# Moving the head products to the end of TensorE's turn in a fused attention and mixture-of-experts layer

## The reference

```python
# attention: 16 query heads of 128, 8 key/value heads, so a key/value head serves a pair of query heads
q = layernorm(x) @ Wq ; k = ctx @ Wk ; v = ctx @ Wv
attn = softmax(where(mask, q @ k.T / sqrt(128), -inf))
x = x + (attn @ v) @ Wo
# feed-forward: 32 experts in 4 groups; the best 2 groups, then the best 4 experts of a row
scores = sigmoid(layernorm(x) @ gate_w.T)
out = sum over the 4 chosen experts of weight * (silu(r @ w1) * (r @ w3)) @ w2, 128 slots for each expert
out = out + (silu(r @ shared_gate) * (r @ shared_up)) @ shared_down
x = x + out
```

## Time and profile before

| | |
|---|---|
| median of 3 runs | 1640.18 us (1640.02 to 1640.26) |
| the profiled execution: its own time | 1641.88 us |
| its span (first to last instruction) | 1639.70 us |
| PE busy | 1604.7 us, 98% |
| DVE, ACT, POOL busy | 1219.1 us, 846.7 us, 797.3 us |
| attention loop, by the first and last `scores` | 17.7 to 1202.5 us |

### The profile page before, as it was taken

The page is one execution under the profiler, slowest core; times in us unless marked ns, Lnnn a source line. Parts: engine busy times, 40 slices in busy tenths (PEclk is TensorE's granted clock), DMA queues, the critical chain, the costliest instruction groups (busy, mean ns, idle before and its releaser), DMA issues. The chain is left out here.

```text
span 1639.7 us, 35025 instructions
## 1 busy us (share of the span) xinstructions
PE 1604.7 (98%) x12199; PEld 1149.5 (70%) x12199; DVE 1219.1 (74%) x3520; ACT 846.7 (52%) x2090; POOL 797.3 (49%) x1096
## 2 busy tenths in 40 slices
PE   8999999999999999999999999999999999999996
PEld 5767777777777777777777677777777666666663
DVE  7988787887778787777887787878766256766773
ACT  6764545454454454454545445445433156666672
POOL 3443646455564646464554646464346433333323
PEclk9999999999999999999999999999999999999999
DMA  8765454454555545445445454444466478988935
GB/s 262 182 155 108 105 97 111 77 112 79 119 96 117 109 86 105 97 111 91 124 81 120 92 117 111 88 111 83 103 215 193 103 208 218 272 244 221 268 67 65
DMA packets 399662, 218.28 MB, mean 133 GB/s; under 512 B 348400, under 2 KB 356592, under 8 KB 399488
## 3 DMA queue, kind: packets, MB, share of 16 engines
q1 hardware_dynamic: 383024, 189.71, 46.6%
q0 software_dynamic: 15904, 25.29, 9.3%
q10 hardware_dynamic: 560, 1.05, 0.2%
HBM read 91.87 MB, written 40.80 MB: 81 GB/s over the span
## 5 line engine op out<-in xcount | busy, mean ns | idle before, releaser
L967 ACT ACTIVATE arena<-arena,neg_max 128x256 f32<-128x256 f32 x512 | 253.7, 496 | 378.4 <-DVE neg_max L1276 378.4
L711 POOL TENSOR_SCALAR arena<-arena,prob_scale 128x256 f16<-128x256 f32 x384 | 185.3, 498 | 478.5 <-DVE prob_scale L1285 436.1
L1648 PE MATMUL ps_query<-xn_both,arena 128*128 128x256 f16 x1024 | 279.2, 273 | 0.7 <-DMA xn_both<-xn_half 0.7
L1650 PE MATMUL ps_query<-xn_both,arena 128*128 128x256 f16 x1024 | 279.2, 273 | 0.0
L1649 PE MATMUL ps_query<-xn_both,arena 128*128 128x256 f16 x1024 | 279.2, 273 | 0.0
L1276 DVE CUSTOM_DVE_ANT_0 arena<-ps_score,mask_add 128x256 f32<-128x256 f32 x512 | 186.3, 420 | 80.8 <-PE ps_score L1650 80.8
L1291 DVE SCALAR_TENSOR_TENSOR arena<-arena,prob_scale 128x256 f16<-128x256 f32 x384 | 239.6, 673 | 7.6 <-POOL arena L711 7.6
L1648 PE MATMUL ps_out<-arena,o_t 128*128 128x512 f16 x512 | 194.2, 379 | 0.6 <-DVE o_t L1296 0.5
L1650 PE MATMUL ps_out<-arena,o_t 128*128 128x512 f16 x512 | 194.2, 379 | 0.0
L1649 PE MATMUL ps_out<-arena,o_t 128*128 128x512 f16 x512 | 194.2, 379 | 0.0
L1296 DVE SCALAR_TENSOR_TENSOR o_t<-ps_head,o_t 128x512 f16<-128x512 f32 x128 | 88.4, 690 | 89.0 <-ACT o_t L980 89.0
(11 more groups left out here) (337 smaller groups left out, 4068.2 us busy)
## 6 DMA issues: line engine op xcount, KB each, us to landing
arena<-w SPq DMA_DIRECT2D x96, 512.0 KB, 6.1
out_rows_dram<-weight_in POOLq DMA_DIRECT2D x32, 256.0 KB, 5.3
x_in<-x SPq DMA_DIRECT2D x15, 512.0 KB, 3.8
out_rows_dram<-x SPq DMA_DIRECT2D x30, 256.0 KB, 2.4
xn_rows<-xn_half SPq DMA_DIRECT2D x15, 512.0 KB, 3.1
x2t_kept<-xn_both SPq DMA_DIRECT2D x12, 512.0 KB, 2.9
ctx_in<-ctx_t SPq DMA_DIRECT2D x16, 256.0 KB, 3.0
weight_in<-wq SPq DMA_DIRECT2D x8, 512.0 KB, 5.0
```

The costliest lines, as they stand in the source:

```text
L711: pool.tensor_scalar(p_rows[:, c, 0, :], probs[:, c, :], prob_scale[:, c:c + 1], 1.0, ALU.mult, ALU.mult).then_inc(norm_hi, 1)
L967: act.activation(probs[:, c, :], probs[:, c, :], ACT.Exp, bias=neg_max[:, c:c + 1], scale=-1.0, accum_out=prob_sum[:, c:c + 1]).then_inc(e ...
L1648: pe.matmul(dst, a.hi, b.hi, start=start and n == 0, stop=False)
L1650: m = pe.matmul(dst, a.lo, b.hi, start=False, stop=stop and n == len(pairs) - 1)
```

## The change

TensorE's turn becomes: `scores(i)`, `query(i + 1, 0)`, filler, `query(i + 1, 1)`, filler, `key(i + 1)`, `project(i - 2)`, `attend(i - 1)`. The loops of PE, ACT and DVE run one turn more to finish the last projection. On DVE the head's low half (`head_low(i - 2)`) comes right behind the maxima, and the low halves of query and key come ahead of `probs_low`, which is no longer cut in two. On ACT `head_high(i - 2)` begins the turn and `query_high` comes ahead of `scale_last`. Side work moves to a later turn, mostly by one: the value tiles to turns 1 to 3, the gate to turn 4, the ranks to turn 7, `turn_xn2` to turn 3. `xn2_rest` moves from ahead of turn 2's `prob_scales` to behind turn 3's `probs_low`. `record(z, 0)` and `record(z, 1)` move from turn 7 and the next item's turn 0 to turns 0 and 1 of the item after it, so that all eight indirect DMAs of item 14 come after the loop.

```diff
@@ def first, def second (fillers; b > 0)
-            if j == 1:
+            if j == 2:
                 return ("value", a, 0, 1) if a < B else None
-            return {3: ("gate", z), 6: ("rank", z)}.get(j)
+            return ("rank", z) if j == 7 and b == B - 1 else None
...
-            if j < 3:
-                return ("value", a, *((0, 0), (1, 0), (1, 1))[j]) if a < B else None
+            if 1 <= j < 4:
+                return ("value", a, *((0, 0), (1, 0), (1, 1))[j - 1]) if a < B else None
+            if j == 4 or j == 7 and b < B - 1:
+                return ("gate" if j == 4 else "rank", z)
             return None
@@ pe_program
-            for i in range(TURNS + 1):
+            for i in range(TURNS + 2):
...
-                else:
-                    piece(1)
-                if i:
-                    attend(i - 1)
                 if i + 1 < TURNS:
                     query(i + 1, 1)
...
                 if i >= TURNS - 1:
-                    piece((i - TURNS + 1) * 2)
-                if i:
-                    project(i - 1)
+                    piece(i - TURNS + 1)
+                if i >= 2:
+                    project(i - 2)
+                if 1 <= i <= TURNS:
+                    attend(i - 1)
@@ act_program
+                if i >= 2:
+                    head_high(i - 2)
                 if i < TURNS:
                     exps(i)
...
-                if i:
-                    head_high(i - 1)
+                if i + 1 < TURNS:
+                    query_high(i + 1)
                 if i < TURNS:
                     scale_last(i)
...
-                if j == 4 and b + 1 < B and i < TURNS:
+                if j == (5 if b else 4) and b + 1 < B and i < TURNS:
                     for t in range(TB):
                         xn_high(b + 1, t)
-                if i + 1 < TURNS:
-                    query_high(i + 1)
...
-                if j == 1 and b and i < TURNS:
+                if j == 3 and b and i < TURNS:
                     for t in range(TB):
                         xn2_high(b - 1, t)
@@ dve_program (the side work's new turns are in the text above)
                 if live:
                     maxima(i)
+                if i >= 2:
+                    head_low(i - 2)
...
+                if i + 1 < TURNS:
+                    query_low(i + 1)
                 if live:
-                    probs_low(i, range(0, CELLS // 2))
...
+                    filler(second(b, j), ps_fill[0])
+                if i + 1 < TURNS:
                     key_low(i + 1)
                 if live:
-                    probs_low(i, range(CELLS // 2, CELLS - 1))
...
+                    probs_low(i, range(CELLS - 1))
...
+                if j == 3 and routed:
+                    for t in range(TB):
+                        xn2_rest(z, t)
...
+                if j == 5 and live and a < B:
+                    xn_rest(a, 0)
+                if j == 5 and routed:
                     choose_5()
                     choose_6()
@@ sync_program
-                if j == 2 and b:
+                if j == 3 and b:
                     for t in range(TB):
                         turn_xn2(b - 1, t)
@@ pool_program
-                if j == 7 and b:
-                    record(z, 0)
                 if j == 0 and b > 1:
+                    record(b - 2, 0)
+                if j == 1 and b > 1:
                     record(b - 2, 1)
...
-            record(z - 1, 1)
+            for t in range(TB):
+                record(z - 1, t)
```

More of the change, by code:

```diff
@@ L792, in pool_program @@
                     halve_ident()
-                if j == 1 and b:
+                if j == 2 and b:
                     inv_std(1, z, x1_stats, x1_rstd, x1_normed)
@@ L1475, in dve_program @@
                 live, routed = i < TURNS, i < TURNS and b > 0
-                if j == 1 and routed:
+                if j == 2 and routed:
                     residual(z, 1)
@@ L1479, in dve_program @@
                     maxima(i)
+                if i >= 2:
+                    head_low(i - 2)
                 for n in split_amid.get(i, ()):
                     weight_low(n)
-                if j == 1 and routed:
+                if j == 0 and b > 1:
+                    dve.wait_ge(*own.now())
+                    pick(position)
+                    find_slots(b - 2)
+                if j == 2 and routed:
                     for t in range(TB):
                         x1_stats_row(z, t)
[L1485 to L1488, removed]
+                if j == (4 if b else 3) and live and a < B:
                     for t in range(TB):
                         x_stats_row(a, t)
-                if j == 4 and routed:
+                if j == 5 and routed:
                     choose_2()
@@ L1494, in dve_program @@
                     choose_4()
-                if j == 5 and routed:
-                    choose_7()
-                    choose_8(z)
                 if j == 6 and live and a < B:
-                    for t in range(TB):
-                        xn_rest(a, t)
+                    xn_rest(a, 1)
                 if j == 7 and routed:
-                    dve.wait_ge(*own.now())
-                    pick(position)
-                    find_slots(z)
+                    choose_10()
+                    choose_11(z)
                 if live:
@@ L1507, in dve_program @@
                     filler(first(b, j), ps_fill[1])
-                else:
-                    piece(1)
                 if i == 0:
                     value_low(ps_fill[1], 0, 0, 0)
-                late_head = live and first(b, j) is not None and first(b, j)[0] == "value"
-                if i and not late_head:
-                    head_low(i - 1)
+                if i + 1 < TURNS:
+                    query_low(i + 1)
                 if live:
-                    probs_low(i, range(0, CELLS // 2))
-                if i and late_head:
-                    head_low(i - 1)
-                if i == 0:
-                    query_low(i + 1)
+                    filler(second(b, j), ps_fill[0])
+                if i + 1 < TURNS:
                     key_low(i + 1)
                 if live:
-                    probs_low(i, range(CELLS // 2, CELLS - 1))
-                if 0 < i < TURNS - 1:
-                    query_low(i + 1)
-                early_key = live and second(b, j) is not None and second(b, j)[0] == "value"
-                if i + 1 < TURNS and early_key:
-                    key_low(i + 1)
-                if live:
-                    filler(second(b, j), ps_fill[0])
-                if 0 < i < TURNS - 1 and not early_key:
-                    key_low(i + 1)
-                if j == 1 and b == B - 1 and live:
+                    probs_low(i, range(CELLS - 1))
+                if j == 2 and b == B - 1 and live:
                     x1_norm(z)
@@ L1559, in dve_program @@
                     ctx_low(b + 2)
-                if j == 0 and b:
-                    residual(z, 0)
             z = B - 1
-            residual(z, 1)
+            for t in range(TB):
+                residual(z, t)
             for t in range(TB):
```

31 lines of the change are left out of this document (16 added, 15 removed).

## The result

The changed kernel takes 1652.32 us (median of 4 runs, 1651.62 to 1653.68), the kernel before 1640.10 on the same chip: a ratio of 1.0076, 95% interval 1.0058 to 1.0093. It is slower, and by more than the 0.2% that can be told from nothing. I had forecast 1634.2.

A forecast was written before the change was run, and what follows sets the result against it. PE, busy for 98% of the span, bounds the kernel, so only its waits count. -11.5 - 3.0 + 3.5 + 3.0 + 2.0 = -6.0 us on 1641.88 gives 1635.9; that execution was 1.7 above the median, so 1634.2; range 1625 to 1644.

The forecast's parts named there:

- The bound now, and what the change takes away: PE's waits in the loop: 11.5 us for late transposes and 3.0 us for late keys at turn 0 would go.
- New waits +3.5: In the loop, late landings at the gate and the chains behind it add 3.5 us, between 0 and +9.
- The gate: Turn 4: operands land at 13.3, wanted at 13.72, slack 0.4; two late landings at 15 gates cost 2.4 us.
- The chain behind SP's queue: Turn 3's probabilities' transposes land at 6.4 in turn 4, wanted at 7.8; attend and DVE's turn 6 chain cost about 1 us.
- the slack of 0.4: Turn 6: DVE's low half of the head ends at 4.2, and the projection wants it at 4.59.
- The signs of being wrong: PE waiting at ps_fill for a DMA in most items, or at ps_out for DVE, or landings late more often.
- DVE's low halves nearer to 470: DVE's low halves of probabilities, mostly behind POOL's work, take near 470 ns each, 1.3 us for three.
- The start, +3.0: Program start: one projection deeper, 2.6 us, plus 0.4 for DVE's catching up in turn 3; between 0 and +4.
- Behind the loop, +2.0: Item 14's eight indirect DMAs on POOL delay the chain to add_shared by 2.0 us, between 0 and 5.2.
- The gate becomes a wait at every item: Rival: xn2_rest's transposes land later, gate stops PE in each of 15 items, 12 us, 1643.8; chance 0.16.
- A blocked DVE: Rival: DVE's choosing steps in turn 5 blocked by POOL's x_norm, 16 us over 15 items, 1650; chance 0.04.
- From 1630 to 1637: Whole kernel: the likeliest case's time span in us, with the bounds of the three costs.

The follow-up runs named there:

- gate_early: Changed kernel with xn2's high halves right behind turn 3's exponentials on ACT and its low halves right behind turn 3's probability scales on DVE; 1634.68 us, ratio 0.9969.
- queue: gate_early with the gate's second transpose on SP held until turn 2's attend ends, its rows' store next, both ahead of turn 3's probabilities' transposes; 1664.08 us.
- head_first: Changed kernel with head_low(i - 2) ahead of maxima(i) on DVE; 1650.35 us, ratio 1.0066.
- warm: Changed kernel with eight matmuls of zeros (512 columns each) at the end of each of PE's first two turns; 1651.80 us, ratio 1.0073.
- tail: Changed kernel with the four indirect DMAs of the first half of item 14's record behind POOL's split of piece 2, not piece 5; 1655.50 us.
- start: gate_early with the low half of weight chunk 7 ahead of turn 1's probs_low on DVE; 1638.89 us, ratio 0.9987.
- tail2: gate_early with the four indirect DMAs of the first half of item 14's record behind POOL's split of piece 1; 1635.74 us, ratio 0.9965.
- shift: Changed kernel with 64 matmuls of 8 columns of zeros ahead of the first key product on PE; 1660.23 us, ratio 1.0111.

## Why the prediction was wrong

**The bound now, and what the change takes away.** Right in kind and size: 11.5 us of waits for transposes and 3.0 of late keys were predicted, and the loop of the kernel before is 14.5 us longer than the dense one of gate_early. That it fits to a tenth is luck: place by place the two come to 10.9 and 2.9, and item 1 has other waits. Scores follow the matmul ahead of them directly at turn 0, and one wait at `ps_head` is left.

**"New waits +3.5", between 0 and +9.** This is the step that failed: they are 17.6 us in the loop, 17.6 - 3.5 = 14.1 of the 15.7 by which the sum missed (+9.7 in place of -6.0). It failed in two parts.

*The gate.* The times on DVE and SP were right to 0.2 us, with a slack of about 0.6 for landings of 2.7. I took two late ones. There are four in 15, and waits that I had not looked for (DVE 0.5 to 0.7 late in items 5, 8 and 12; item 15, whose turn 3 has no filler): 9.0 us in place of 2.4. Each item offers two transposes, and a late one costs 1.3 to 1.7.

*The chain behind SP's queue.* I wrote that the probabilities' transposes of turn 3 land at 6.4 in turn 4 and that `attend` wants them at 7.8. The engine that matters is POOL, which may not overwrite their source before. For `x_norm` I allowed for a delay of this kind (not before 9.3 + 1.3 in turn 4, where an ordinary turn has POOL through at 7.3), and for nothing else. DVE's low halves of turn 4 wait for POOL too, and behind them the gate's evaluation and the maxima of turn 5: this path I had not followed. Nor had I followed a late landing along it. With none, and DVE in time, POOL starts 6.6 to 6.9 into turn 4, much as my 6.4 says; in the six items with a landing of over 4 us it starts at 7.7 to 8.6, and the median of all is 7.6. In turn 6 the slack of 0.4 was not there: the projection waits 0.2 to 0.5 in 11 items, and the scores in 5. The chain cost 8.8 us in place of "about 1". queue shows that the delay on SP is enough to make these waits, head_first that swapping the two steps at their end only moves them.

**The signs of being wrong.** One that I had named came: landings are late more often than before, 41 against 27 over 4 us (last section).

**"DVE's low halves nearer to 470."** Too low: the median is 610 ns, from 684. POOL's halves and DVE's still overlap in most turns. It did not hurt the gate (`xn2_rest` starts 8.3 into turn 3, forecast 8.4), but it stands in the chain of turns 4 and 5 above, where three took 1.84 us at 892.82. POOL's first high half came a little later than forecast too: in turn 4 of gate_early 4.9 to 5.7 and not 4.6 to 4.7.

```profile
L1293 DVE SCALAR_TENSOR_TENSOR arena<-arena,prob_scale x384: 471/610/910, 25.6 to 1212.6; 128x256 f16<-128x256 f32 x192
```

**The start, +3.0.** 4.3 (2.6 for the projection, 1.7), a little over the upper bound. Scores of turn 3 start at 45.56 and not near 44: DVE's weight chunk 7 stands behind low halves that now come in one piece. The drop of the clock beside it costs next to nothing (warm, tail), and moving the chunk only moves the gap (start).

**Behind the loop, +2.0.** 2.3, by the mechanism named: the eight DMAs, PE's wait of 2.4 at piece 12, and the wait near 1294 at 4.0 as forecast.

**The rivals.** "The gate becomes a wait at every item" (1643.8) was the right side but the wrong shape: it is a wait at half of the items, and as much again comes from the queue behind it. "A blocked DVE" (1650) is near in time and wrong in cause. Beside POOL's `x_norm`, DVE's `beats` took 0.19 us as it does elsewhere, but the step ahead of it, `group_score`, was held for a short time:

```profile
896.39 4.13 POOL L682 TENSOR_SCALAR weight_in<-x_in,mean_var,rstd 128x512 f32<-128x512 f32 x2
...
898.65 0.58 DVE L1324 TENSOR_TENSOR group_score<-group_top 128x8 f32<-128x8 f32 x1
899.27 0.19 DVE L1330 TENSOR_TENSOR beats<-group_score 128x32 f32<-128x32 f32 x1
```

In the 14 items where it starts 0.19 to 0.26 us after the second instruction of `x_norm` it takes 0.52 to 0.59, and each time it ends 0.78 after the start of that one; in the kernel before, where it starts 0.9 us or more after it, it takes 0.17. So 0.4 us of DVE went there in turn 5, behind the maxima and the head's half of that turn and ahead of its scales, and not up to 1.6; in gate_early the same happens in three items and no wait follows. The rule of the Trainium skill (SBUF — State Buffer, "Who interferes with whom"), by which the later one is blocked until the first is finished, is borne out by neither row: POOL's instruction runs for 2.07.

**A bound that was worked out wrongly.** "From 1630 to 1637" does not follow from the bounds of the three costs. They give 1640.2 - 14.5 = 1625.7 and, with 18.2 added, 1643.9, which is the range that I stated at the end.

**The order itself.** gate_early is the change with two steps of side work placed elsewhere, and it takes 1634.68 us. So the moved products do win what I had counted; the side work's new place gave it away. gate_early and tail2 beat the kernel before, by 0.3% each, and the changed one by about 1%.

## What to carry to other kernels

When a transfer is queued behind another one, list everyone who waits for its landing, not only the product that reads it: the engine that may not overwrite its source comes first here. Follow a late start through every turn until the chain has slack again, since the loss comes out one or two turns later, on another engine. And place a transfer whose operands are ready early where the queue is idle; two steps moved forward by 4 us within a turn were worth 18 us.

## What the runs showed of the hardware

Transposes that land late are, for the most part, not chance. Packets of the queue that the page calls "q8 instruction" carry 16 KB each (page of the kernel before):

```profile
q8 instruction: 99, 1.62, 0.4%
```

They come every 16 us. Over the 317 landings that I could match in the kernel before, 26 of the 27 that took over 4 us had such a packet in their flight, against 14 of the 290 others. In shift, with 128 PE instructions more, there are 100. In the changed kernel the window 583 to 589 of item 7 has one, beside the transposes that were late:

```profile
q8 instruction: 1, 0.02, 1.8%
```

The same stretch of item 6 has none, and there the gate's transposes landed after 2.8. In the changed kernel 23 of 41 late landings have such a packet, so other causes are there too (loads and stores now follow the transposes directly, which no run tests), and only shift, where the late landings moved with the packets, and not a count, speaks for cause and not mere company.

On the second chip the kernels start, tail2, queue and shift lose 3 to 4 us at the keys of turn 2, and tail2's loop is 1096.86 us against 1093.79 of gate_early, whose loop code is the same. In turn 2 DVE's third row of maxima starts 0.6 to 2.4 us behind the second there in 3 to 7 items, where 0.34 is usual, while POOL issues its record; no other trace has this. What causes it is open.
